# Regrouping the turns on TensorE in an attention and mixing loop: side, x and maxima moved beside the other whole-array products, the mix one step later

## The reference

```
# token layer: F = 32, I = 512, H = 256
hid = silu(x_cat @ W_h.T + b_h)
h = hid @ W_o.T + b_o + x_cat @ W_r.T + b_r
# attention: 16 heads of 16 numbers, q, k, v with one 16 x 16 matrix each
xh = layernorm(h)
energy = einsum('bqhd,bkhd->bhqk', q, k) / sqrt(256)
h = h + (softmax(energy) @ v) @ W_out.T + b_out
# spectral mixing
x_freq = fft(layernorm(h))
y = real(ifft(einsum('bnd,do->bno', x_freq, w)))
h = h + y + bias
```

## Time and profile before

| what | value |
|---|---|
| median of 3 runs | 141.29 us (141.2 to 141.3) |
| the profiled execution's own time | 141.65 us |
| its span, first to last instruction | 139.8 us |
| granted TensorE clock over the span | 1.000 |
| busy: PE, PEld | 132.5 us (95%), 111.9 us (80%) |
| busy: DVE, POOL, ACT | 112.0 us (80%), 94.9 us (68%), 85.8 us (61%) |
| DMA | 5.89 MB, mean 42 GB/s |

### The profile page before, as it was taken

The page is one execution under the profiler, slowest core; times in us unless marked ns, Lnnn a source line. Parts: engine busy times, 40 slices in busy tenths (PEclk is TensorE's granted clock), DMA queues, the critical chain, the costliest instruction groups (busy, mean ns, idle before and its releaser), DMA issues.

```text
span 139.8 us, 6135 instructions
## 1 busy us (share of the span) xinstructions
PE 132.5 (95%) x2444; PEld 111.9 (80%) x2444; DVE 112.0 (80%) x337; ACT 85.8 (61%) x245; POOL 94.9 (68%) x186
## 2 busy tenths in 40 slices
PE   6679999999999998999999999999999999999991
PEld 2269999999998877878889888788888887887650
DVE  5574697949978597798898988988989889879671
ACT  4374766567888395847748659477476494663410
POOL 3285795997574455587696876876867868764751
PEclk9999999999999999999999999999999999999999
DMA  3678000021000011112203213123032031122012
GB/s 70 157 171 249 31 0 0 0 28 19 2 0 5 5 9 14 19 42 23 56 8 61 46 15 61 40 23 65 2 59 51 10 61 42 19 55 50 3 38 75
DMA packets 24508, 5.89 MB, mean 42 GB/s; under 512 B 20384, under 2 KB 24224, under 8 KB 24480
## 3 DMA queue, kind: packets, MB, share of 16 engines
q1 hardware_dynamic: 24192, 5.37, 18.3%
q10 hardware_dynamic: 288, 0.13, 0.3%
HBM read 2.35 MB, written 2.10 MB: 32 GB/s over the span
## 4 chain that ended last, share of the span: by engine, by line
PE 83%; DVE 6%; DMA 3%; issue 2%; POOL 1%; ACT 1%; SPq 1%; DVEq 0%
PE bank L1054 11%; PE bank L972 11%; PE bank L1040 7%; PE bank L1096 6%; PE bank L1116 6%; PE bank L977 5%; PE bank L1103 4%; PE bank L1149 4%; PE bank L1084 4%; DMA wf_raw<-in_W_r 3%; PE bank L1067 2%; PE bank L1162 2%; PE bank L966 2%; PE bank L1120 2%; PE bank L1153 2%
## 5 line engine op out<-in xcount | busy, mean ns | idle before, releaser
L829 DVE TENSOR_REDUCE bank<-bank 128x4 f32<-128x256 f32 x64 | 22.8, 425 | 6.9 <-ACT pT L378 6.4
L378 ACT ACTIVATE pT<-bank 128x256 f32<-128x256 f32 x64 | 19.4, 389 | 2.5 <-PE bank L1067 2.5
L1054 PE MATMUL bank<-qT,xzT 32*128 32x64 f32 x512 | 17.9, 276 | 0.0
L1054 PEld LDWEIGHTS bank<-qT,xzT 32*128 32x128 f32 x512 | 15.7, 186 | 2.7 <-issue 2.7
L700 DVE TENSOR_TENSOR hid_lo<-bank,hid_hi 128x512 fp32r<-128x512 f32 x16 | 11.0, 686 | 7.2 <-ACT bank L346 7.2
L587 POOL TENSOR_TENSOR side_lo<-sideT,side_hi 128x256 fp32r<-128x256 f32 x14 | 10.2, 729 | 8.1 <-ACT sideT L389 8.1
L548 POOL TENSOR_SCALAR xblk<-xh,parity_sb 128x128 f32<-128x128 f32 x32 | 11.6, 375 | 5.8 <-PE bank L1103 4.7
L373 ACT ACTIVATE maxT<-bank 128x128 fp32r<-128x128 f32 x16 | 4.4, 277 | 17.8 <-PE bank L1076 17.8
L598 POOL TENSOR_TENSOR on_lo<-onT,on_hi 128x256 fp32r<-128x256 f32 x14 | 10.3, 737 | 7.1 <-ACT on_hi L393 6.9
L556 POOL TENSOR_TENSOR hb_all<-h_all,bout_bc 128x256 f32<-128x256 f32 x16 | 11.6, 738 | 4.0 <-ACT h_all L350 4.0
L341 ACT ACTIVATE hid_hi<-bank 128x512 fp32r<-128x512 f32 x16 | 9.6, 598 | 4.2 <-PE bank L966 4.1
(11 more groups left out here) (170 smaller groups left out, 386.1 us busy)
## 6 DMA issues: line engine op xcount, KB each, us to landing
out<-y SPq DMA_DIRECT2D x16, 128.0 KB, 1.7
xblk<-xh SPq DMA_DIRECT2D x32, 32.0 KB, 2.5
wo_raw<-in_W_o SPq DMA_DIRECT2D x1, 512.0 KB, 4.3
wout_raw<-in_W_out SPq DMA_DIRECT2D x1, 256.0 KB, 3.0
fr<-in_wr SPq DMA_DIRECT2D x1, 256.0 KB, 4.4
fi<-in_wi SPq DMA_DIRECT2D x1, 256.0 KB, 4.6
minus_raw<-in_minus_rows SPq DMA_DIRECT2D x1, 128.0 KB, 2.1
bout_bc<-in_b_out SPq DMA_DIRECT2D x1, 128.0 KB, 3.5
```

The costliest lines, as they stand in the source:

```text
L378: nc.scalar.activation(pT[:, j, :], bank[j][:, D:2 * D], ACT.Exp).then_inc(exp_done, 1)
L829: nc.vector.tensor_reduce(rowmax[:, j, :], bank[j][:, 0:D].rearrange("p (h k) -> p h k", k=TOK), AX_X, ALU.max).then_inc(max_done, 1)
L1054: pe.matmul(bank[j][:, at0:at0 + TOK], xzT[t % 3][rows32, 2 * half + b, :, :].rearrange("p e k -> p (e k)"), qT[t % 3][rows32, half, TOK * ...
```

## The change

It reorders the loop and frees what the new order needs.

- PE's step i becomes: `scores` of i + 2, `keyed_scores` and `take_max` of i + 1, `mix_freq` of i - 2, `query` of i + 3, side of i - 1, `project` of i, x of i + 4, maxima of i + 2, `weigh` of i + 1. All turns stand between whole-array products. The maxima of i + 2 are turned before `weigh` of i + 1 and not after it, x is turned one tile further ahead, and the mix is one step later.
- ACT's step becomes: `copy_xzT`, `lead_on`, `exponent`, `copy_q`, `copy_side`, `copy_xT` of i + 4, `copy_max` of i + 2.
- DVE splits `variance2` (`h2_stats` ahead of the maxima, the rest behind them) and takes `split_x` ahead of it; `finish` is one step later.
- POOL's step becomes: `place_same`, `add_bias`, `split_on`, `normalize` of i + 5, `split_side`, `inv_std2`. SP stores y two steps later in its order.
- `xh` has three buffers in place of two. The turned side lies in the left half of bank 5 (which `weigh` writes) and only for the last two tiles in the right half of bank 6. So `turn_side` waits for `on_set`, and `weigh` waits for `side_copied`.
- `WHOLE_ON` goes from 14 to 15: tile 14 is projected with six products of split terms too.
- `project` of tile 14 waits for `y_set` of tile 12, whose `finish` is moved ahead of `residual` in that DVE step.

```
-WHOLE_ON = 14
+WHOLE_ON = 15
...
-        xh = [sb(f"xh{i}", [P, D]) for i in range(2)]
+        xh = [sb(f"xh{i}", [P, D]) for i in range(3)]
...
+        def side_of(t):
+            return bank[PV_BANK][:, 0:D] if t < T - 2 else bank[MAX_BANK][:, D:2 * D]
...
             def step(i):      # ACT
-                if i + 1 < T:
-                    copy_max(i + 1)
-                if i >= 1:
-                    copy_side(i - 1)
                 if i + 3 < T:
-                    copy_xT(i + 3)
                     copy_xzT(i + 3)
                 if i < WHOLE_ON:
                     lead_on(i)
...
                 if i + 3 < T:
                     copy_q(i + 3)
+                if i >= 1:
+                    copy_side(i - 1)
+                if i + 4 < T:
+                    copy_xT(i + 4)
+                if i + 2 < T:
+                    copy_max(i + 2)
...
+                if 1 <= i < T:      # POOL, after place_same(i + 2)
+                    add_bias(i - 1)
+                if i < WHOLE_ON:
+                    split_on(i)
+                if i + 5 < T:
+                    normalize(i + 5)
                 if 1 <= i <= WHOLE_SIDE:
                     split_side(i - 1)
...
+                if i >= 1:
                     inv_std2(i - 1)
...
             def step(i):      # DVE
                 divide(i)
-                if i >= 1:
-                    variance2(i - 1)
                 if i + 3 < T:
                     split_x(i + 3)
+                if i >= 1:
+                    h2_stats(i - 1)
                 if i + 2 < T:
                     for j in range(QUADS):
                         maximum(i + 2, j)
                     split_max(i + 2)
+                if i >= 1:
+                    variance2(i - 1)
+                if i == T - 2:
+                    finish(i - 2)
                 residual(i)
-                if 1 <= i < T - 2:
-                    finish(i - 1)
+                if 2 <= i < T - 2:
+                    finish(i - 2)
...
             def turn_side(t):
                 pe.wait_ge(h2_done, t + 1)
+                if t < T - 2:
+                    pe.wait_ge(on_set, t + 2)
...
             def weigh(t):
...
+                if t >= 2:
+                    pe.wait_ge(side_copied, t - 1)
...
             def project(t):
...
+                if t == T - 2:
+                    pe.wait_ge(y_set, t - 1)
...
             def step(i):      # PE
-                if 0 <= i + 2 < T:
+                if i + 2 < T:
                     scores_inputs(i + 2)
...
+                    scores(i + 2)
...
+                keyed_scores(i + 1)
+                take_max(i + 1)
+                if i >= 2:
+                    mix_freq(i - 2)
+                if i + 3 < T:
                     query(i + 3)
...
+                turn_side(i - 1)
+                project(i)
+                if i + 4 < T:
+                    turn_x(i + 4)
+                if i + 2 < T:
+                    turn_max(i + 2)
+                weigh(i + 1)
```

More of the change, by code:

```diff
@@ L304, in _ @@
             place_crossed(1)
-            for i in range(T + 1):
+            for i in range(T + 3):
                 if i + 2 < T:
                     place_crossed(i + 2)
-                if i >= 1:
-                    store(i - 1)
+                if i >= 3:
+                    store(i - 3)
             for par in range(2):
@@ L444, in _ @@
             lead_mix_weights()
+            copy_xT(3)
+            copy_max(1)
             for i in range(T + 1):
@@ L604, in step @@
                     split_mix_weights()
+                if 1 <= i < T:
[4 more added lines that the diff above has]
+                    normalize(i + 5)
                 if 1 <= i <= WHOLE_SIDE:
                     split_side(i - 1)
-                if i < WHOLE_ON:
-                    split_on(i)
-                if i >= T - 1:
+                if i == T:
                     add_bias(i - 1)
+                if i >= 1:
                     inv_std2(i - 1)
[L612 to L616, removed]
             EARLY = T // 2 + 2
@@ L641, in _ @@
             inv_std1(3)
+            normalize(4)
             for i in range(T + 1):
@@ L920, in _ @@
             divide(T - 1)
+            h2_stats(T - 2)
             variance2(T - 2)
@@ L923, in _ @@
             residual(T - 1)
+            h2_stats(T - 1)
             variance2(T - 1)
@@ L1083, in turn_side @@
                 for half in range(HALF):
-                    last = pe.transpose(bank[SIDE_BANK][:, D + half * P:D + (half + 1) * P],
+                    last = pe.transpose(side_of(t)[:, half * P:(half + 1) * P],
                                         h2[t % 2][:, half * P:(half + 1) * P], ident[:])
@@ L1111, in mix_freq @@
                     pe.wait_ge(mix_split, 1)
+                    pe.wait_ge(h2_done, 2)
                 if t >= 1:
@@ L1161, in turn_x @@
                 for half in range(HALF):
-                    last = pe.transpose(bank[X_BANK][:, half * P:(half + 1) * P], xh[t % 2][:, half * P:(half + 1) * P],
+                    last = pe.transpose(bank[X_BANK][:, half * P:(half + 1) * P], xh[t % 3][:, half * P:(half + 1) * P],
                                         ident[:])
@@ L1257, in _ @@
             cols_spectrum(0)
-            for i in range(-1, T - 1):
+            turn_max(0)
+            scores_inputs(1)
+            scores(1)
+            keyed_scores(0)
+            take_max(0)
+            query(2)
+            cols_spectrum(1)
+            weigh(0)
+            turn_x(3)
+            turn_max(1)
+            scores_inputs(2)
+            scores(2)
+            keyed_scores(1)
+            take_max(1)
+            query(3)
+            project(0)
+            turn_x(4)
+            turn_max(2)
+            weigh(1)
+            for i in range(1, T - 1):
                 step(i)
```

51 lines of the change are left out of this document (17 added, 34 removed).

## The result

The changed kernel takes 150.7 us (median of four runs, 150.01 to 150.89) beside 141.3 us (141.2 to 141.5) for the kernel before on the same chip: a ratio of 1.066, interval 1.063 to 1.068. I had forecast 148.2 and a range up to 150.2. The sign is right, the time lies outside the range. The profiled execution took 150.89 us with a span of 149.1.

What follows compares the result with a forecast made beforehand. PE's own instructions were taken to bound the kernel at 5.56 us a step; the added wait makes it 5.94. Step terms sum to +6.87 us: 141.29 + 6.87 = 148.2 us, 8-in-10 range 144.6 to 150.2.

Steps and rivals of the forecast that it cites:

- step 0: First loop step: exponentials held by `take_max`, then the turn of tile 2's maxima joins; 6.27 in place of 4.92, +1.35 us.
- step 1: Second loop step: 5.94 in place of 6.01 us, -0.07.
- steps 2 to 12, ring: The eleven full steps: each lasts the 5.94 us chain sum, 65.34 in place of 61.17 us, +4.17.
- step 13: Next-to-last loop step: 5.94 in place of 4.99 us, +0.95; the missing `query` does not help since PE waits anyway.
- step 14: Last loop step: `project` of 14 waits for `y` of 12; 4.80 us, +0.47, bounds 4.33 and 5.1.
- the ring after: Between two `weigh` starts: `divide`, `on_hi`, exponentials, reductions, split and turn must fit; 5.94 us, 0.38 above the present step.
- Two changes of form saved: On PE: fewer whole-array/tiled switches, counted as one saving of 0.20 us a step (bounds 0 and 0.40), leaving 5.36 for PE alone.
- PE can't pass the waiting turn: At `turn_max`: PE pulls no later weight load past it, so the full 0.30 us counts; otherwise a step of about 5.7.
- the wait that I had called met: At `weigh`: its new wait for `side_copied` costs nothing, as both side copies follow `copy_q`, by 5.4 us.
- A: Rival: maxima are in time and PE saves 0.20 us a step in the loop; 137.8 us; chance 5%.
- B: Rival: exponentials are held by `take_max` alone, not `on_hi`; 5.68 us a step, +3.49, 144.8 us; chance 11%.
- C: Rival: POOL or the landing of the crossing DMAs takes the lead, 0.25 us a step more over 14 steps; 151.7 us; 5%.

## Why the prediction was right in its sign and short in its size

The table sets its terms against what was measured (spans and windows, us; the tails are 9.04 before and 9.03 after):

| term | forecast | measured |
|---|---|---|
| up to the first `weigh` | 0 | -0.63 |
| step 0 | +1.35 | +1.20 |
| step 1 | -0.07 | -0.20 |
| steps 2 to 12, ring | +4.17 | +2.75 (63.92 - 61.17) |
| steps 2 to 12, supply of instructions and half clock | 0 | +4.61 (68.53 - 63.92) |
| step 13 | +0.95 | +0.82 |
| step 14 | +0.47 | +0.74 |
| sum | +6.87 | +9.29 |

- **PE bound by its own instructions before; the ring after.** Right. With the turn behind `weigh` again the wait is gone, with `on_hi` out the step falls to the next ring (5.65, through `take_max`), with the exponentials first `project` waits instead, and with the turn alone moved the old order has a loss too, though by the ring through `take_max`. Every hop is where it was forecast.
- **The ring's length, 5.94 against 5.81: mis-sized.** The hop from `on_hi` to the exponential measured 0.32, not 0.41: I took it from a row where `on_hi` lasted 0.46, and it lasts 0.42 when ACT comes to it from idleness. The turn to the next load is 0.26, not 0.30. The rest is a hundredth each. Over the 14 steps this is 1.8 us too much.
- **Two changes of form saved, 0.20 us.** Right, as far as estimates tell: 5.56 - 5.40 = 0.16 in the whole, 0.23 between the two orders. I had 5.36 for PE alone. The ring hides it, so it does not enter the sum.
- **PE can't pass the waiting turn.** Right: the load at 117.58 stands behind the waiting turn at 117.32, 0.26 later, in every step of 5.81.
- **Step 14, 4.80 against 5.07.** The wait for `y` of tile 12 came as drawn (3.94 after `weigh`, I had 3.84). Behind it I took 0.90 for the projection and the change of form; it took 1.13:

```profile
138.95 0.39 PE L1174 MATMUL bank<-value_hi,on_hi 128*128 128x256 f32 x1 [0.46 <-DVE y L879]
...
139.52 0.42 ACT L393 ACTIVATE sideT<-bank 128x256 f32<-128x256 f32 x1
...
140.08 0.42 PE L1118 MATMUL bank<-pT,pair_ones_sb 128*32 128x256 f32 x4 [0.16 <-ACT sideT L393]
```

  The last `weigh` waited for the side's copy, the wait that I had called met. It is met in a full step of 5.81; this step has no maxima to hide it.
- **What was missing, and broke the range: the supply of instructions.** The sum has no term for it. I had read that the clock was 1.00 and that no row of step 9 waited for an engine, and took this to say that PE can always run its own stream. It said so for this stream with this placing of its instructions. Nothing of the forecast looked at the queue of kind "instruction", though the page of before has it too. The 4.6 us are more than the whole error of +2.4 us; the ring's error of -1.8 and the earlier first `weigh` hid the rest. With the supply in time the changed kernel takes 146.56 us, inside my range and 1.6 below my forecast. That the forecast came as close as 2.5 us is luck: two errors had opposite signs. The first `weigh` started between 48.7 and 49.7 us in the kernels here with at most 58 idle products more, 48.73 in one with them, so I do not put the -0.63 in the table down to the change.
- **Rivals.** A, the gain, falls: PE needs 5.40, the ring 5.81. B is not what happened, since `on_hi` is on the ring, but its ring is only 0.16 shorter. C did not lead: PE's weight loads stood twice for POOL's `xh`, 0.8 us together in steps 0 and 1, and the maxima came later still.

Open: why the refill starts one `weigh` later once the boundary has been among the whole-array products of the new order. It is not PE's waiting at the maxima alone (with the turn behind `weigh` the gaps are there, and in the old order with the turn ahead they are not), and not the waits of `weigh`. Both orders that show it have `scores` directly or nearly behind `weigh` and the mix, the query, the side and the projection in one stretch; the old order, which catches up with a second refill in one step (at 4.06 in step 2 of the kernel before, at 4.29 in that order with the turn moved ahead), has not. Whether that is the cause was not tried.

## What to carry to other kernels

A turn that moves ahead of a stage closes a ring through everything its operand needs: add the hops from that stage back to itself, and compare the sum with the engine's own need, not with the wait that is there today. Look for the next longest ring too, since shortening the first pays only down to it. Take each hop from a row where the engine was in the same state, idle or busy. And where a change rewrites the order of a stream of small products, look for idle time on "issue" inside a group of equal ones, and repeat the run with a few dozen idle instructions ahead: if the time moves, part of the difference belongs to the placing of the instructions and not to the order.

## What the runs showed of the hardware that I had not expected

- PE's instructions come in packets of 16 KB, by my count for 256 of them. In this kernel PE went on from its gaps at the boundary 2.3 to 2.8 us after a packet had started, in the variants 2.3 to 2.9. The gaps were 0.5 to 1.5 us, and with the half clock behind one of them cost 4.6 us of 150.7 here.
- A gap can cost twice. Behind gaps of 1.47 us (this kernel), 1.30, 1.02 and 1.01 us (three of the variants), the granted clock fell to 0.50 for 3.41 us; behind others of 1.01 us (this kernel, and the one shifted by 214) and of 1.17 us (the one with the waits moved) it did not.
- 58 and 30 more idle products at the start, 40 us ahead of the loop, changed the time of the same kernel from 150.7 to 146.6 and 147.8 us, and 107 of them to 152.9 (2.5 of it a later start of the loop).
